# AdaLN-conditioned FFN in float32: the first bias loaded by columns instead of turned on TensorE, and thirteen opening matmuls on ones instead of fifteen

## The reference

```python
W = weights[condition]                         # one 64x64 matrix for each of 32 batches
u = jnp.einsum('bct,bcd->bdt', x, W)           # x: (32, 64, 1024)
h = jax.nn.gelu(jnp.einsum('bsd,df->bsf', u, inter_w) + inter_b, approximate=True)
out = jnp.einsum('bsf,fd->bsd', h, output_w) + output_b
return x + out                                 # inter_w (1024, 4096), output_w (4096, 1024)
```

## Time and profile before

| what | value |
|---|---|
| median of 3 runs | 1260.7 us (1260.35 to 1261.21) |
| profiled execution, its own time | 1260.64 us |
| span of that execution in the trace | 1258.8 us |
| PE busy | 1253.7 us (100%), 5664 matmuls |
| DVE, ACT, POOL busy | 825.6 us (66%), 566.9 us (45%), 188.1 us (15%) |
| chain that ended last, by engine | PE 97%, DVE 1%, DMA 1% |
| DMA moved | 249.28 MB, mean 198 GB/s |

### The profile page before, as it was taken

The page is one execution under the profiler, slowest core; times in us unless marked ns, Lnnn a source line. Parts: engine busy times, 40 slices in busy tenths (PEclk is TensorE's granted clock), DMA queues, the critical chain, the costliest instruction groups (busy, mean ns, idle before and its releaser), DMA issues.

```text
span 1258.8 us, 15370 instructions
## 1 busy us (share of the span) xinstructions
PE 1253.7 (100%) x5664; PEld 1043.1 (83%) x5664; DVE 825.6 (66%) x1087; ACT 566.9 (45%) x969; POOL 188.1 (15%) x95
## 2 busy tenths in 40 slices
PE   9999999999999999999999999999999999999998
PEld 9888888888888888888888888888888888888887
DVE  5977787676577777657655455554547767784764
ACT  4845454454544444444434444444444444444442
POOL 4362223321000000000034233312200000000000
PEclk9999999999999999999999999999999999999999
DMA  9586655764997322349835224544189932223431
GB/s 343 160 275 244 242 196 222 283 250 177 384 392 283 97 89 99 101 165 360 310 137 195 95 119 174 184 184 145 74 330 396 351 132 93 101 101 100 155 131 51
DMA packets 94090, 249.28 MB, mean 198 GB/s; under 512 B 7328, under 2 KB 15552, under 8 KB 92608
## 3 DMA queue, kind: packets, MB, share of 16 engines
q1 hardware_dynamic: 93408, 248.14, 54.6%
q10 hardware_dynamic: 576, 0.15, 0.1%
q0 software_dynamic: 32, 0.00, 0.0%
HBM read 162.28 MB, written 85.98 MB: 197 GB/s over the span
## 4 chain that ended last, share of the span: by engine, by line
PE 97%; DVE 1%; DMA 1%; SPq 0%; POOL 0%; ACT 0%; issue 0%; ACTq 0%; DVEq 0%
PE ps L580 48%; PE ps L564 48%; DMA w_raw<-in_L_ffn_inter_w_dram 1%; PE ps L517 1%; POOL s_w L476 0%; SPq L321 0%; DVE y_whole L795 0%; DVE acc L878 0%; DVE lhs L800 0%; DVE y_whole L782 0%; DVE y L789 0%; SPq L318 0%; ACT lhs L646 0%; ACT y_stage L623 0%; SPq L317 0%
## 5 line engine op out<-in xcount | busy, mean ns | idle before, releaser
L564 PE MATMUL ps<-y,lhs 128*128 128x512 f32 x2688 | 611.4, 389 | 0.0
L580 PE MATMUL ps<-rhs,lhs 128*128 128x512 f32 x2688 | 609.6, 389 | 0.0
L580 PEld LDWEIGHTS ps<-rhs,lhs 128*128 128x128 f32 x2688 | 504.7, 188 | 104.6
L564 PEld LDWEIGHTS ps<-y,lhs 128*128 128x128 f32 x2688 | 504.2, 188 | 104.3
L716 ACT ACTIVATE lhs<-h_raw 128x512 fp32r<-128x512 f32 x224 | 141.6, 632 | 345.8 <-PE ps L580 340.2
L859 DVE TENSOR_TENSOR lhs<-h_raw,lhs 128x512 fp32r<-128x512 f32 x224 | 155.0, 692 | 188.5 <-ACT lhs L716 188.5
L800 DVE TENSOR_TENSOR lhs<-w_raw,lhs 128x512 fp32r<-128x512 f32 x128 | 111.1, 870 | 131.6 <-ACT lhs L646 131.5
L646 ACT ACTIVATE lhs<-w_raw 128x512 fp32r<-128x512 f32 x128 | 80.9, 633 | 171.7 <-PE ps L564 165.2
L862 DVE TENSOR_TENSOR rhs<-W,rhs 128x512 fp32r<-128x512 f32 x224 | 153.3, 684 | 0.0
L800 DVE TENSOR_TENSOR lhs<-s_w,lhs 128x512 fp32r<-128x512 f32 x96 | 91.3, 953 | 89.3 <-ACT lhs L646 89.1
L468 POOL TENSOR_TENSOR s_w<-w_raw 128x1024 f32<-128x1024 f32 x16 | 48.9, 3055 | 620.3 <-PE ps L580 354.0
(11 more groups left out here) (38 smaller groups left out, 290.1 us busy)
## 6 DMA issues: line engine op xcount, KB each, us to landing
h_raw<-h_mem SPq DMA_DIRECT2D x112, 512.0 KB, 3.3
w_raw<-in_L_ffn_inter_w_dram SPq DMA_DIRECT2D x32, 1024.0 KB, 8.6
h_mem<-hs SPq DMA_DIRECT2D x64, 512.0 KB, 4.5
W<-in_L_ffn_output_w_dram SPq DMA_DIRECT2D x32, 1024.0 KB, 12.4
h_mem<-c SPq DMA_DIRECT2D x48, 512.0 KB, 5.4
y_mem<-y_out SPq DMA_DIRECT2D x28, 512.0 KB, 3.5
y<-y_mem SPq DMA_DIRECT2D x7, 2048.0 KB, 12.8
acc<-in_x_dram SPq DMA_DIRECT2D x16, 512.0 KB, 9.0
```

The source lines that it names most:

```text
L564: last = nc.tensor.matmul(ps[:, bank, :], w[:, k, :], y[i][:, part, k, :], start=(i in FRESH and k == 0 and u == 0), stop=(k == KH - 1 and ...
L580: last = nc.tensor.matmul(ps[:, bank2(h, j, tb), :], lhs[s % RING][:, a, blk(tb)], rhs[r][:, w, :], start=(j in FRESH and q == 0 and u == ...
```

## The change

Two edits. The bias is loaded by one DMA straight into `b1_col`, issued by SP behind the eight loads of x1; the 32 rows, the identity, the matmul and the copy are gone, and with them the wait of `cond1(1)`. ACT waits for the DMA ahead of its GELUs of chunks 10 and 11. The activation that loads the GELU table early now reads `ones` instead of the identity. And `WARM` is 13 instead of 15.

```diff
-    WARM = 15
+    WARM = 13
...
                 sp.dma_start(x1[j][:], x_tok[1, :, j, :]).then_inc(x1_in[j], 16)
+            with nc.allow_non_contiguous_dma(reason="one column of 32 values a partition"):
+                sp.dma_start(b1_col[:], b1.rearrange("(a p) -> p a", p=P)).then_inc(b1_in, 16)
...
-            nc.gpsimd.memset(ident[0:F // P], 0.0).then_inc(ident_zero, 1)
-            pool.wait_ge(ident_zero, 1)
-            nc.gpsimd.affine_select(out=ident[0:F // P], in_=ident[0:F // P], compare_op=ALU.not_equal, fill=1.0, base=0,
-                                    pattern=[[-1, F // P]], channel_multiplier=1).then_inc(ident_made, 1)
...
-                if j == 1:
-                    pe.wait_ge(b1_ready, 1)
...
-            def turn_b1():
-                pe.wait_ge(b1_in, 16)
-                pe.wait_ge(ident_made, 1)
-                pe.wait_ge(kept_dve, KB)
-                nc.tensor.matmul(ps[:, 7, 0:F // P], b1_rows[0:F // P], ident[0:F // P],
-                                 start=True, stop=True).then_inc(b1_turned, 1)
...
-                        if (h, g, c) == (0, 0, 0):
-                            turn_b1()
...
                 if c in (10, 11):
                     p = c - 10
+                    act.wait_ge(b1_in, 16)
                     act.wait_ge(c12_added, 2 * n + p + 1)
...
-            act.dma_start(b1_rows[0:F // P], b1.rearrange("(a p) -> a p", p=P)).then_inc(b1_in, 16)
-            act.wait_ge(ident_made, 1)
-            nc.scalar.activation(table_ahead[0:F // P, 0:1], ident[0:F // P, 0:1], ACT.Gelu_apprx_tanh)
+            act.wait_ge(ones_made, 1)
+            nc.scalar.activation(table_ahead[:, 0:1], ones[:, 0:1], ACT.Gelu_apprx_tanh)
...
-            dve.wait_ge(b1_turned, 1)
-            nc.vector.tensor_copy(b1_col[:], ps[:, 7, 0:F // P]).then_inc(b1_ready, 1)
             y_low(1)
```

More of the change, by code:

```diff
@@ L102, in build @@
         b2_all = at("b2_all", 216, [D])
-        b1_rows = at("b1_rows", 220, [P])
         b1_col = at("b1_col", 220.5, [F // P])
-        ident = at("ident", 220.75, [F // P])
         itok_sb = at("itok_sb", 221, [B], I32)
@@ L135, in build @@
         picked1 = sem("picked1")
-        ident_zero = sem("ident_zero")
-        ident_made = sem("ident_made")
         s_made = [sem(f"s_made{i + 1}") for i in range(4)]
         t_made = [sem(f"t_made{i + 1}") for i in range(4)]
-        b1_turned = sem("b1_turned")
         cond_done = sem("cond_done")
@@ L156, in build @@
         y1_hi = sem("y1_hi")
-        b1_ready = sem("b1_ready")
         kept_dve = sem("kept_dve")
```

## The result

Over 22 executions each, the changed kernel took 1263.34 us in the median (1261.34 to 1265.55) and the kernel before 1261.01 us (1260.16 to 1262.38). The medians differ by 2.3 us. The ratio on record is 1.0016, with a 95% interval of 1.0010 to 1.0023: slower by 0.16%, with the median outside my range of 1259.4 to 1262.4. The spread of the changed kernel is twice as wide, 4.2 us against 2.2, which a cost that is always paid would not do. The page is that of the longest of the 22 executions, 1265.55 us.

What follows compares the result with a forecast made beforehand. The prediction took the kernel as bound by PE's unbroken work from cond1(2) at 36.79 us, a start set by ACT's copy. From 1260.64 us it took 0.02 and 0.03, giving 1260.6, range 1259.4 to 1262.4.

Steps and rivals of the forecast that it cites:

- What bounds the kernel: PE is busy without a gap from cond1(2) at 36.79 us; ACT's copy, ending at 36.66, sets that start.
- The new DMA, cost 0: DMA queue from 32 us: 4096 4-byte packets at 9 to 17.5 ns fit a 5.4 us hole, delaying nobody.
- The rival of the slow packets: DMA queue from 32 us: packets over 32 ns delay ACT's copy of part 3, then PE; 9 in 100 above 0.2%.
- The estimate of 43 us: DMA queue: at the skill page's 10.5 ns per packet, 4096 packets take 43 us and ACT stands about 35 us.
- DVE's copy, gain 0 to 0.03 us: DVE at 26.77 us: without the bias copy the low part of y starts 0 to 0.03 us sooner; 0.02 taken.
- The turning matmul, gain 0: PE at 23.99 us: saves 0.40 us, but PE then idles some 0.8 us instead of 0.41 before cond1(2).
- My clock rival: Opening and idle near 6 us: slow pace returns, costing PE 1.6 us, 0.8 felt (5 in 100); large form 2 in 100.
- The two opening matmuls, gain 0: PE's opening: free 0.43 us sooner, but x0 lands at 6.47 us, so the first real matmul still begins at 6.55.
- the longer idle ahead of the first real matmul: Sign of being right: PE idles 0.62 us instead of 0.19 before the first real matmul at about 6.5 us.
- The sum: Whole kernel: 1260.64 less 0.02 for DVE's copy and 0.03 for ACT's load of the rows gives 1260.6 us.
- the 0.2% to which I gave 87 in 100: Whole kernel: time stays within 0.2%, or 2.5 us, of the kernel before; 87 in 100, slower 12, faster 1.

Runs made afterwards that it cites:

- a_warm13: The kernel before with 13 opening matmuls instead of 15, bias still turned on PE; median 1261.39 us, ratio 0.9999.
- b_cols15: The changed kernel with 15 opening matmuls instead of 13, so bias by columns alone; median 1261.59 us, ratio 1.0005.
- d_before: The kernel before, unchanged, measured again for a second profile; median 1261.51 us, ratio 1.0001.
- q_order: The changed kernel with 15 or 13 opening matmuls, POOL's second sum of group 0 also waiting for DVE's first half-difference; medians 1260.94 and 1260.77 us.
- o_dma_only: The kernel before with the new bias DMA added into a spare tile, ACT waiting for it, nothing removed; median 1261.07 us, ratio 1.0000.
- f_copy: The changed kernel with DVE's copy from PSUM back in its old place and cond1(1) waiting for it; median 1261.94 us, ratio 1.0005.
- n_late: The changed kernel with four matmuls of cond1(7) done twice, at about 62 us; median 1262.58 us, ratio 1.0008.
- w11: The changed kernel with 11 opening matmuls instead of 13; median 1262.05 us, ratio 1.0008.
- c_again: The changed kernel, unchanged, measured again for a second profile; median 1261.95 us, ratio 1.0005.
- h_early: The changed kernel with ACT's copies of parts 0 and 1 moved ahead of its high part of the second difference; median 1259.69 us, ratio 0.9987.
- q_order13: The changed kernel, 13 opening matmuls, with POOL's second sum of group 0 also waiting for DVE's first half of the second difference; median 1260.77 us, ratio 1.0004.
- e_fill: The changed kernel with four matmuls of cond1(1) done twice, ahead of the idle before cond1(2); median 1261.72 us, ratio 1.0002.
- h15_early: The changed kernel with ACT's copies of parts 0 and 1 moved ahead and 15 opening matmuls; median 1259.78 us, ratio 0.9987.
- q_order15: The changed kernel, 15 opening matmuls, with POOL's second sum of group 0 also waiting for DVE's first half of the second difference; median 1260.94 us, ratio 1.0000.

## Why the prediction was wrong, by its steps

*What bounds the kernel*: right. In the 13 profiles of the table ACT's copy sets the start of `cond1(2)`, and in before, a_warm13, b_cols15, d_before and both q_order kernels the span ends 1222.0 us behind it (0.1 us either way).

*The new DMA, cost 0*: right, and shown by `o_dma_only`. It was through by 35 us, inside the hole, as 9 to 17.5 ns a packet had it. The rival of the slow packets, to which most of my chance for slower went, did not happen. The estimate of 43 us worked out from the Trainium skill, page "DMA: Bandwidth & Descriptors", section "Measured", does not hold for this transfer, which was through within 5 us.

*DVE's copy, gain 0 to 0.03 us*: this is the step that failed, for the part of the loss that the runs explain best. I priced the instruction and asked what starts sooner, not whom its neighbours meet. The earlier trace rows showed POOL's sum at 4.47 us where the profile's page of before has a mean of 2.62 for this line, and I read it as a length, not as half of a turn-taking that can fall the other way. Without the copy it fell the other way in all ten profiles: about +0.85 us at `cond1(2)`, 0.5 to 1.2 us of the lowest time given back by the wait in the q_order kernels. As the kernel before pays it in some executions too (three of six profiles with the copy), its share in the difference of medians is smaller, and `f_copy`, with the copy back, recovered the lowest time and the early order but not the median. Why a copy of 0.18 us ahead of three other instructions decides the turn is open: in before and after POOL starts 0.16 us behind the first half alike.

*The turning matmul, gain 0*: right as far as it goes. I wrote that PE would stand 0.8 us instead of 0.41; in the profiles of the change and of b_cols15, n_late and w11 it stood 1.26 to 1.99 us. I treated this idle as free. It is free only while the clock holds. In the profile after it was followed by the lower clock, which cost 1.63 us in `cond1(2)` and `cond1(3)` and 3.0 us with what followed. My clock rival gave 1.6 us too, but that agreement is luck: it priced the slow pace of the opening's 18 records, looked for the gap at 6 us instead of here, and had no second idle. By the clocks on record at most nine of the 22 executions had this cost.

*The two opening matmuls, gain 0*: right for PE's start; a_warm13 is at 0.9999. The working was off in one place. The 1.00 that the earlier trace rows gives for the clock of the opening is no reading: the trace of before has no record of the clock ahead of 4.47 us, and the pace goes from 0.20 to 0.107 us a record at that moment, at 4.53. In the profile after both come later, at 5.9, so the 26 records took 5.38 us where 30 had taken 5.16, and the longer idle ahead of the first real matmul, which I had named as a sign, is not there. Across all profiles the moment lies between 4.4 and 7.4 us, in kernels with 15 as with 13. It cost nothing, since PE waits for ACT at `cond1(2)` all the same.

But with the two matmuls four records and four weight loads go from PE's instruction stream, and with the turning matmul two more of each. My sum had no term for the instruction loads. In three of the seven profiles with 11 or 13 opening matmuls and no doubled ones a 16 KB instruction load falls on the last stores (c_again, h_early, w11), for 1.8 to 2.05 us. In the other four (after, a_warm13, f_copy, q_order13), in the nine profiles with 15 and in e_fill and n_late it does not. The number of PE's instructions alone does not place it: in after it comes 3.1 us ahead of the start of DVE's last additions and in c_again, the same kernel, 3.2 us behind it. That the load makes those executions long is shown in the three profiles; that it makes the whole upper group is argued from the numbers: 4 of 11 in c_again and q_order13, 3 of 11 in w11, one in h_early, none in a_warm13, e_fill, n_late, h15_early and q_order15, and one, at 1265.19, in b_cols15.

*The sum*: it predicted 1260.6 for 1263.34. That the ratio, 1.0016, still lies within the 0.2% to which I gave 87 in 100 is no merit of the working, since each term in it had the loss at nothing. The lower group of c_again is at 1261.4 to 1262.1, where +0.85 us puts it. That the rest of the 2.3 us comes from executions with one of the two other costs, the lower clock (at most nine of 22) and the instruction load, is argued and not shown: only one of the 22 has a profile. How they divide stays open. So does why on the chip of c_again the medians differ by 0.5 us only, and whether the first weights, which landed later in some profiles of the changed kernel, add to it.

The version to take is the one with ACT's copies moved ahead, the bias by columns and 15 opening matmuls: 1259.78 us, 0.9987 (0.9978 to 0.9996) of the kernel before, with no idle before `cond1(2)` and no long end in its profile, and no execution over 1260.82. Against the kernel before with the same copies moved ahead (1260.38, 0.9995) its lead is not clear of noise.

## What to carry to other kernels

When an instruction is removed from DVE, look at what POOL does in the next few us (here the copy at 26.77 and POOL's sum at 30.50): a POOL or DVE instruction that takes 1.7 times the mean of its line (4.47 against 2.62 us) or nearly three times its twin (3.43 against 1.22) marks a turn that can fall either way, and the one on the critical chain should be made to win it by an explicit wait, or taken off the chain by moving work of the waiting engine ahead. Work taken from PE ahead of a stall is not neutral: the stall gets longer, and behind a long one the clock can fall (here behind 1.84, 3.09 and 3.84 us, not behind 1.83 and 1.99). Compare the lowest execution and the groups of a set, not only the median; a wider spread after a change is a finding, and its causes are found in profiles of the long executions, of which one is not enough. And measure the change a second time before explaining all of it: here 2.3 us became 0.5.

## What the runs showed that I had not expected

- 4096 packets of 4 bytes passed within 5 us, with the DMA engines' share at 59.6% over them, and partly between the last packets of x1.
- One 16 KB instruction load on one DMA engine takes 1.6 us between the last stores of c_again (0.96 us for several of the earlier ones), and the run ends 1.8 to 2.05 us later in the three profiles that have one there. The Trainium skill, page "Runtime: NRT & Kernel Launch", section "Instruction fetch mechanics", calls the cost of crossing the boundary of such a block mostly hidden. The profile's page of before counts 46 packets on queue 8, and none shows on its chain of waits: the trace agrees. In the three profiles of other kernels the last of them was not hidden.
- A DVE instruction that meets POOL's lasts up to 3.43 us instead of 1.22, and which of the two gives way changed between executions of one and the same kernel (0.8 us).
